# First stage of a decoder kernel: six weight loads are issued behind a wait for two Gram banks

## What is computed

```python
x = x + _L0_attn_ref(_layernorm(x))             # plain attention across the 16 batch rows
x = x + _L0_xattn_ref(_layernorm(x), ctx, mask, Wq, Wk, Wv, Wo, q_norm_w, k_norm_w)   # 32 heads of 128, 8 key heads
x = x + _L0_ffn_ref(_layernorm(x), gate_w, bias, Wg, Wu, Wd, Sg, Su, Sd)              # 16 experts, top 4, one shared

def _L0_attn_ref(x):                            # x: (16, 64, 512)
    q = jnp.transpose(x, (2, 0, 1))             # for each of 512 columns l a 16 x 64 matrix
    scores = jnp.einsum('lnc,lmc->lnm', q, q) / x.shape[1] ** 0.5   # a 16 x 16 Gram matrix per column
    prob = jax.nn.softmax(scores, axis=-1)
    return x + jnp.transpose(jnp.einsum('lnm,lmc->lnc', prob, q), (1, 2, 0))
```

## Time and profile before

| | |
|---|---|
| time, median of 3 runs | 809.94 us (808.97 to 810.89) |
| the profiled execution | 809.31 us |
| its span, first to last instruction | 807.5 us |
| PE / PEld busy | 96% / 55% |
| DVE / ACT / POOL busy | 73% / 64% / 67% |
| mean granted TensorE clock | 0.993 |

### The profile page before, as it was taken

The page is one execution under the profiler, slowest core; times in us unless marked ns, Lnnn a source line. Parts: engine busy times, 40 slices in busy tenths (PEclk is TensorE's granted clock), DMA queues, the critical chain, the costliest instruction groups (busy, mean ns, idle before and its releaser), DMA issues.

```text
span 807.5 us, 21596 instructions
## 1 busy us (share of the span) xinstructions
PE 777.2 (96%) x7887; PEld 445.1 (55%) x7887; DVE 591.6 (73%) x1023; ACT 516.8 (64%) x968; POOL 543.3 (67%) x428
## 2 busy tenths in 40 slices
PE   6789999999999999999999999999998999999997
PEld 2664545645645655655654654654554565665653
DVE  5787795595685686777667668699688776767778
ACT  3898987487587587587578578636433566555551
POOL 6953496896896986976977978872253656565433
PEclk9799999999999999999999999999999999999999
DMA  8029516516507507516515524436515557678894
GB/s 329 18 95 290 164 67 235 143 53 227 165 26 234 164 18 238 168 36 229 158 55 188 176 79 151 124 113 248 177 52 209 199 182 248 219 282 277 264 401 183
DMA packets 50661, 138.94 MB, mean 172 GB/s; under 512 B 6176, under 2 KB 8224, under 8 KB 46240
## 3 DMA queue, kind: packets, MB, share of 16 engines
q1 hardware_dynamic: 43600, 116.93, 43.6%
q0 software_dynamic: 6400, 20.98, 7.6%
q10 hardware_dynamic: 592, 0.08, 0.1%
HBM read 96.02 MB, written 39.85 MB: 168 GB/s over the span
## 4 chain that ended last, share of the span: by engine, by line
PE 62%; POOL 13%; issue 8%; DVE 5%; DMA 5%; ACT 4%; SPq 2%; DVEq 0%; POOLq 0%; ACTq 0%
PE ps L1742 33%; PE ps L2192 18%; POOL ring_mem L623 4%; DMA stage<-in_wq 3%; POOL reg_h L661 3%; POOL ring_mem L609 2%; PE ps L2182 2%; POOL reg_h L665 2%; PE ps L1961 2%; POOL ring_mem L616 1%; PE ps L2253 1%; PE ps L1947 1%; PE ps L2207 1%; DMA w_split<-stage 1%; PE ps L1902 1%
## 5 line engine op out<-in xcount | busy, mean ns | idle before, releaser
L1742 PE MATMUL ps<-wo_hi,reg_b 128*128 128x512 f16 x448 | 142.5, 379 | 1.0 <-DVE x_res L1336 1.0
L2192 PE MATMUL ps<-ring_mem,reg_h 128*64 x480 | 116.6, 379 | 4.1 <-DVE kv L1639 2.3
L703 POOL DMA_INDIRECT y_rows<-reg_h,to_row x40 | 66.7, 1669 | 77.3 <-ACT reg_h L1115 71.6
L661 POOL TENSOR_SCALAR reg_h<-reg_h 128x512 f32<-128x512 f32 x56 | 95.4, 1704 | 33.2 <-ACT reg_h L913 33.0
L2194 PE MATMUL ps<-kv,reg_h 128*64 128x512 f16 x480 | 116.7, 380 | 0.0
L665 POOL TENSOR_TENSOR reg_h<-reg_h 128x512 f16<-128x512 f32 x84 | 108.7, 1294 | 4.7
L1742 PE MATMUL ps<-hT_hi,wq_hi 128*128 128x512 f16 x256 | 97.2, 380 | 2.0 <-DVE ring_mem L1279 1.8
L1742 PE MATMUL ps<-hT_hi,wq_lo 128*128 128x512 f16 x256 | 97.2, 380 | 0.0
L1742 PE MATMUL ps<-hT_lo,wq_hi 128*128 128x512 f16 x256 | 97.1, 379 | 0.0
L623 POOL TENSOR_TENSOR ring_mem<-kv,ring_mem 128x512 f16<-128x512 f32 x64 | 80.3, 1255 | 24.2 <-ACT ring_mem L838 24.2
L1742 PE MATMUL ps<-wo_lo,reg_b 128*128 128x512 f16 x224 | 85.0, 379 | 0.0
(11 more groups left out here) (343 smaller groups left out, 2019.2 us busy)
## 6 DMA issues: line engine op xcount, KB each, us to landing
ring_mem<-w_split SPq DMA_DIRECT2D x16, 1536.0 KB, 7.7
w_split<-reg_h SPq DMA_DIRECT2D x88, 256.0 KB, 2.1
reg_h<-in_wgu SPq DMA_DIRECT2D x58, 256.0 KB, 3.6
stage<-in_wq SPq DMA_DIRECT2D x8, 1024.0 KB, 8.9
stage<-in_wo SPq DMA_DIRECT2D x8, 1024.0 KB, 6.6
reg_h<-in_wd SPq DMA_DIRECT2D x30, 256.0 KB, 3.1
wkv_st<-in_wkv SPq DMA_DIRECT2D x8, 512.0 KB, 9.5
ring_mem<-in_x_half SPq DMA_DIRECT2D x8, 256.0 KB, 6.1
```

Of the source, the lines that this page charges most:

```text
L661: pool.tensor_scalar(st, st, WS, None, ALU.mult).then_inc(pre_scaled_pool, 1)
L703: pool.indirect_dma_start(y_rows, bass.IndirectOffsetOnAxis(ap=to_row[:, r - 1:r], axis=0), y[r % 2], None).then_inc(scattered[r % 2], 16)
L1742: last = pe.matmul(dst, lhsT(c), rhs(c), start=(m == 0), stop=(m == n - 1))
L2192: pe.matmul(dst[0:TS, :], x[:, 0:TS], ring[:, bass.ds(at + w, BANK)], start=(first and n == 0), stop=(stop and n == 2))
```

## The change

The query weights' load moves behind that of the key and value weights, and both, with the four loads of expert units behind them, move behind a wait for two finished Gram banks.

```diff
             sp.dma_start(ctx_st, ctx_t.rearrange("p (k t) -> p k t", k=KC)).then_inc(ctx_in, 16)
+            sp.wait_ge(gram, 2)
+            sp.dma_start(wkv_st[:, :, :], wkv[0]).then_inc(wkv_in, 16)
             sp.dma_start(wq_st, wq[0]).then_inc(wq_in, 16)
-            sp.dma_start(wkv_st[:, :, :], wkv[0]).then_inc(wkv_in, 16)
             for q in range(SLOTS):
                 sp.dma_start(first_st[q], wgu[0, :, q, :]).then_inc(pre_in[q], 16)
```

## The result

| | before | changed |
|---|---|---|
| median | 810.25 us (807.5 to 814.71) | 814.75 us (811.15 to 817.96) |
| ratio, changed to before, with its 95% interval | | 1.0054 [1.0043, 1.0066] |
| the profiled execution | 809.31 us | 817.96 us |
| its mean granted TensorE clock | 0.993 | 0.987 |

The change costs 0.54%, about 4.4 us. I had forecast 809.6, with a range up to 811.4. What happened is the third rival: a new stop of TensorE in Gram bank 3, for which I had asked 812.0 and a chance of 0.12. The page of the changed kernel, against the earlier trace rows: as many instructions and as many packets of them, a longer span.

The account below looks back on a forecast made before the run. The prediction took ScalarE to bound the first stage. A gain of 0.6 us in bank 1 and a cost of 0.25 us in bank 3 gave -0.35 us, so 809.94 became 809.6 us, range 807.7 to 811.4.

Parts of the forecast that it names:

- The bound, and that it goes straight through to the end: First stage: its time is ScalarE's, and what it gains or loses there moves the end by the same amount.
- The stop as the end of an instruction block: Gram bank 1: TensorE's 1.87 us stop is a wait for its next 16 KB block of instructions.
- The loads held it up by 0.6 us: Gram bank 1: moving 2.5 MB of loads away shortens TensorE's stop, a gain of 0.6 us, bounds 0 and 1.87.
- D: Gram bank 3: delay of TensorE's instruction fetch behind the moved loads, taken as 1.2 us, cost 0.25 us.
- D - 0.95 us: Gram bank 3: cost of a fetch late by D; nothing below 0.95 us, spare at the fetch, VectorE and ScalarE's wait.
- 8 packets of 0.3 us: Gram bank 3: the fetch waits at most for one run of wq packets, 2.4 us, so cost at most 1.45 us.
- Rival 3: Gram bank 3: the stop moves there, the fetch waiting for wkv and wq runs, D 3.6 us; 812.0 us, chance 0.12.
- Nothing for the order, the wait on SyncE and the later landing: The six loads: reordering, waiting and landing by about 33 us cost nothing, with 9 us of cover before ScalarE needs wkv.
- x: VectorE's early waits for the loads of x: no gain expected; at most 1.9 us, given 1 in 20.
- The clock: TensorE: a shorter stop may keep the clock up, bank 2 up to 1.9 us sooner; ScalarE gains only its 0.3 us.

Follow-up runs that it names:

- c1: Kernel before, with TensorE's first 16 transposes ahead of Gram bank 1 and eight later ones behind it: 814.17 against 813.01 us, ratio 1.0011.
- r1: The changed kernel again, beside the kernel before on the same chip: 816.01 against 813.01 us, ratio 1.0047.
- r2: The changed kernel with all six loads waiting for four Gram banks instead of two, run beside r1: 812.86 against before's 813.01 us, ratio 0.9998.
- e5: The changed kernel with 17 instead of 27 dummy matmuls ahead of the Gram banks: 814.71 against before's 811.13 us, one run.
- e1: The kernel before with only the order changed, wkv loaded ahead of wq, no wait: 811.38 against 810.54 us, ratio 1.0016.
- e2: The changed kernel with all six loads waiting for four Gram banks instead of two: 809.52 against before's 810.54 us, ratio 0.9994.
- e6: The changed kernel with the four expert units issued ahead of wkv and wq: 812.08 against before's 811.13 us, ratio 1.0013.
- x1: Kernel before with wkv ahead of wq, then eight 256 KB loads (2 KB packets) behind a wait for two banks: 811.21 against 811.04 us, ratio 1.0009.
- e7: The changed kernel with one more 1 MB load between wq and the expert units: 811.75 against before's 811.13 us, ratio 0.9997.
- e8: The changed kernel with the expert units behind a second wait, for four banks: 811.79 against before's 811.13 us, ratio 0.9994.
- r3: The edit of e7 again, run beside r1: 814.58 against before's 813.01 us, ratio 1.0020.

## Why the prediction was wrong, step by step

**The bound, and that it goes straight through to the end: right as far as can be told.** From the Ln to the end of the span all profiles but one take 750.4 to 754.2 us (c1's takes 757.4), in no order by what was lost ahead of it; but that spread is as large as the effect. r1 and r2 differ in the median by what ScalarE's stretch gives and 0.4 us.

**The stop as the end of an instruction block: right, and now shown** (e5). The Trainium skill, page "Runtime: NRT & Kernel Launch", section "Instruction fetch mechanics", gives blocks of 16 KiB and 256 instructions, which the counts of e5 and e1 bear out. Its rule that this fetch is hidden does not hold here: the stop of 1.3 to 2.0 us in bank 1 is in the profile of every kernel that keeps the order of TensorE's work.

**"The loads held it up by 0.6 us": wrong.** I took the difference between two distances of one profile, 1.29 against 0.60 us, for an effect of the load queue. With no load in flight the stop was 1.74 (e2) and 1.82 us (r2), and in the changed kernel 1.52 and 1.39 (r1). In the nine profiles with no load for 4 us and more ahead of it the stop is 1.4 to 1.9 us and the packet starts 1.3 to 1.7 us after bank 0 does; in the kernel before, behind a queue 98.3% busy, these are 1.87 and 1.74. So the loads made that packet at most 0.4 us late, not 0.6, and a gain in the stop can't be told from its own spread. Its size comes out without traffic. In e1 the packet starts 1.53 us after bank 0 does and TensorE goes on 2.61 us after that, 4.14 together; but 2.40 us after the start of bank 0 it is at the end of its instructions. That leaves 1.74.

**D, the delay in the new place: the step that failed.** The cost formula was D - 0.95 us. Its form is right (a late packet, some spare time, the rest one for one), its number only roughly. Against r2, r1 has a lag longer by 3.57 us, the formula gives 2.6, and the stretches differ by 2.7, but with two effects of the clock that happen to cancel. In the first pair D is 3.2, the formula gives 2.3, and the stretch lost 3.6; the clock explains 1.15 of that (0.57 ahead of bank 3 and 0.58 in it). Over the eight kernels with a stop of 1.9 us and more the stretch lost from 1.0 us less to 1.5 us more than the formula gives. One part of the 0.95 was misread: the 0.27 us of ScalarE's wait was no spare time, since ScalarE waits there for the probabilities of bank 2, which VectorE computes behind the shift of bank 3. A later bank 3 lengthens that wait (1.75 us in the changed kernel); behind bank 3 only 0.15 us were spare, not 0.50. What was off most was D: I expected 1.2 us and bounded it at 2.4, by "8 packets of 0.3 us". It measured 3.2 to 4.1 in the kernels with this wait and these six loads behind it (changed, r1, e6, e5). The scale came from the 0.6 us above, most of which was spread; and the picture behind it, a wait for the run of packets that is being served, is false, as x1 gives 2.9 us with packets of 2 KB alone, where that picture allowed 0.6. So a number that was mostly spread, turned into a rule about packets, made the bound too low. The rule of descriptors in groups, cited beside it from the Trainium skill, page "DMA: Bandwidth & Descriptors", section "Queues, rings and completion order", had made me wary of the right place for a reason that the runs don't bear out.

**Rival 3** named the place, the sign and the sign in the profile ("issue" in bank 3 of over 1 us, VectorE idle before its last shift). Its chance of 0.12 came from "two whole runs in a row would have to go first", which is a statement about the false picture. Its D of 3.6 us is close to the measured 3.2 by luck, since it was added up from runs of packets too; and its 812.0 is 2.75 us short of the median, for it took off a gain in bank 1 that didn't come and left out the clock. Without the picture, the only row that showed a fetch under loads was at a place where it was late already, and D would have had to stay open well past 3 us.

**Nothing for the order, the wait on SyncE and the later landing: right.** e1 and r2 (all six loads later still) equal before; ScalarE comes to `wkv` without a wait (49.29 above). **x: right**, it came no sooner: in the changed kernel's profile the statistics were swapped at 12.96, before at 12.53.

**The clock: half right.** Where bank 3 ends early enough, a lower clock ahead of it costs nothing (e2, r2); where a stop has used up the spare time, what the clock does to banks 2 and 3 shows in full, 1.15 us in the changed kernel's profile.

**Left open.** The stretch explains 2.7 us (r1 against r2) to 3.6 (first pair) of a loss of 3.0 to 4.5 in the medians; what is left over lies in parts that also spread between profiles of equal kernels. The medians don't follow the stop from kernel to kernel: e6, e7, e8 and x1 have stops of 1.9 to 3.3 us in their profiles and stretches 1.0 to 4.2 us longer, yet their medians are 0.2 to 1.0 us over before's, none of it clear of noise. The stop is known from one execution of each kernel only. So r1 against r2 shows the cost of this change and what takes it away; that any kernel with such a stop loses as much isn't shown. And what sets D, 2.3 to 4.1 us, isn't known: it isn't the packets' size (x1), not all that is queued (e7, r3), and not the mere presence of loads, for the packet of 20.65 before came at most 0.4 us late behind a busy queue. Whether the 16 KB come late because of the packets on one of the DMA engines can't be read, for the profile doesn't say which engine carries them.

## What to carry over

Look for 16 KB packets on an instruction queue in the profile, note how long after the previous end of block they start, and keep bulk loads from being in flight at that moment unless the engine has long instructions until the next block: here a wait for bank 2 cost 3.0 to 4.5 us and a wait for bank 4 nothing that could be told. When a bounding engine idles early in a stage, move its later work there, and don't delay the loads which that needs. And don't turn a difference of half a microsecond in one profile into the scale for another cost before a run shows that it is no spread.

## What the runs showed of the hardware

- TensorE's instructions come in packets of 16 KB for 128 matmuls and 128 weight loads. One rule fits every stop in bank 3 of 0.4 us or more, to within 0.2 us: lag + 2.4 us from the start of the packet to the next matmul - 4.1 us from the start of bank 2 to the 14th product of bank 3. It gives 0.4 for e1 (0.46 measured), 2.2 for x1 (2.11), 2.6 for the changed kernel (2.63), 3.0 for r1 (2.93). With a lag of 1.0 to 1.5 and nothing else moving, the fetch is hidden with 0.2 to 0.7 us to spare; in bank 1, where no transposes stand between, it was in no profile here.
- With loads in flight behind the wait for bank 2 the third packet starts 2.3 to 4.1 us later than in quiet kernels, while the packet itself isn't longer: 0.96 to 1.02 us in all kernels with the long lag, against 0.96 to 1.48 in the quiet ones. The engine goes on 2.2 to 2.4 us after it starts. The delay is ahead of the data, not in it.
- The granted clock can fall to 1.2 GHz within the first 20 us or not, in kernels whose TensorE program is the same; the 27 dummy matmuls then take 7.4 to 8.8 us instead of 5.99. That spread is larger than the effect that was sought, and it hides in any single profile.
